# Second SwiGLU and Fourier stage as one pipeline over groups of two batches, with a packed real transform and products on GpSimd

## The reference

```python
# feed-forward of layer 1: SwiGLU, hidden size 384 (weights dequantised by 1/127)
gate = jnp.einsum('bsd,hd->bsh', x, wg)
up = jnp.einsum('bsd,hd->bsh', x, wu)
h = jax.nn.silu(gate) * up
return jnp.einsum('bsh,dh->bsd', h, wd)
...
# attention of layer 2: over frequencies; it adds its own (normalised) input again
fk = jnp.fft.rfft(k, axis=-1)
fk = fk / (jnp.abs(fk) + EPS)
fq = jnp.fft.rfft(q, axis=-1)
fq = fq / (jnp.abs(fq) + EPS)
fv = jnp.fft.rfft(v, axis=-1)
fkv = jnp.cumsum(fk * fv, axis=-2)
values_hat = jnp.fft.irfft(fkv * jnp.conj(fq), n=D, axis=-1)
return x + values_hat
```

## Time and profile before

| what | us |
|---|---|
| median of the runs | 2327.8 |
| lowest and highest of 3 runs | 2325.37, 2330.94 |
| time of the profiled execution | 2331.32 |
| its span | 2329.6 |
| its granted clock, mean | 0.954 |
| the second SwiGLU and the Fourier stage in it | 816.9 to 1038.7 |

### The profile page before, as it was taken

The page is one execution under the profiler, slowest core; times in us unless marked ns, Lnnn a source line. Parts: engine busy times, 40 slices in busy tenths (PEclk is TensorE's granted clock), DMA queues, the critical chain, the costliest instruction groups (busy, mean ns, idle before and its releaser), DMA issues. The chain is left out here.

```text
span 2329.6 us, 66565 instructions
## 1 busy us (share of the span) xinstructions
PE 2085.3 (90%) x21573; PEld 1237.6 (53%) x21573; DVE 1814.9 (78%) x4556; ACT 1460.6 (63%) x3730; POOL 695.9 (30%) x1221
## 2 busy tenths in 40 slices
PE   5999999987899887756999999999999888888798
PEld 4777777755355454542545555555555444444355
DVE  7878877755689647986889998899999877776564
ACT  3565555632488723322878888888888777777331
POOL 2111111100343101322434434434433355552110
PEclk9999999998799988776999999999999999999899
DMA  5000000000434100003343443444344333331000
GB/s 164 2 2 2 2 2 2 2 1 15 137 124 128 40 1 1 1 0 97 121 129 124 129 131 124 128 132 131 128 129 132 113 98 111 98 102 53 1 19 19
DMA packets 198398, 167.48 MB, mean 72 GB/s; under 512 B 15445, under 2 KB 178198, under 8 KB 198198
## 3 DMA queue, kind: packets, MB, share of 16 engines
q1 hardware_dynamic: 198198, 164.90, 22.4%
HBM read 85.42 MB, written 77.63 MB: 70 GB/s over the span
## 5 line engine op out<-in xcount | busy, mean ns | idle before, releaser
L831 DVE TENSOR_REDUCE a_rowmax<-a_psS 128x2 f32<-128x512 f32 x1536 | 964.1, 681 | 141.4 <-PE a_psS L596 137.0
L754 ACT ACTIVATE a_probs<-a_psT 128x512 f32<-128x512 f32 x1536 | 830.5, 601 | 228.9 <-PE a_psT L603 228.8
L596 PE MATMUL a_psS<-stackk,stackq 49*128 49x256 bf16 x3072 | 498.2, 278 | 46.6 <-DMA stackq<-a_negmaxT 14.2
L603 PE MATMUL a_psT<-stackq,stackk 51*128 51x256 bf16 x3072 | 481.9, 273 | 2.1 <-ACT a_probs L754 1.9
L645 PE MATMUL a_psO<-a_probs,values 128*32 128x256 f32 x6144 | 412.8, 386 | 1.4 <-ACT a_probs L754 1.4
L596 PEld LDWEIGHTS a_psS<-stackk,stackq 49*128 49x128 bf16 x3072 | 220.1, 95 | 296.8 <-DVE a_rowmax L831 116.5
L645 PEld LDWEIGHTS a_psO<-a_probs,values 128*32 128x32 f32 x6144 | 160.8, 109 | 144.8 <-issue 51.2
L1175 ACT ACTIVATE a_probs<-a_psS,a_negmax 128x256 f32<-128x256 f32 x256 | 121.1, 473 | 182.8 <-DVE a_negmax L1199 182.8
L603 PEld LDWEIGHTS a_psT<-stackq,stackk 51*128 51x128 bf16 x3072 | 216.9, 94 | 19.3 <-ACT a_probs L754 8.1
L1059 POOL TENSOR_TENSOR a_vr<-a_v,a_rsum 128x256 f32<-128x256 f32 x128 | 79.8, 623 | 392.3 <-DVE a_rsum L1260 371.9
L953 POOL COPY a_xcur<-xT 128x256 f32 (+1 forms) x80 | 31.7, 396 | 467.8 <-ACT values L778 371.7
(11 more groups left out here) (305 smaller groups left out, 3892.6 us busy)
## 6 DMA issues: line engine op xcount, KB each, us to landing
a_scratch<-a_parts SPq DMA_DIRECT2D x192, 192.0 KB, 2.4
stackq<-a_scratch SPq DMA_DIRECT2D x192, 192.0 KB
stackk<-a_scratch SPq DMA_DIRECT2D x192, 192.0 KB
a_scratch<-a_parts SPq DMA_DIRECT2D x192, 128.0 KB, 2.3
a_scratch<-a_parts SPq DMA_DIRECT2D x192, 64.0 KB, 1.9
stackq<-a_negmaxT SPq DMA_DIRECT2D x192, 8.0 KB
x<-in_x SPq DMA_DIRECT2D x4, 512.0 KB, 6.4
out<-x SPq DMA_DIRECT2D x8, 256.0 KB, 2.3
```

The lines of the kernel that those rows point to most:

```text
L596: return pe.matmul(psS[score_bank(s, u)[0]][:, t * SEQ:(t + 1) * SEQ], stackq[r:r + MAX_ROW, b, pr, t * P:(t + 1) * P], stackk[r:r + MAX_R ...
L603: return pe.matmul(psT[shifted_bank(s, u)[0]][:, t * SEQ:(t + 1) * SEQ], stackk[r:r + ZERO_ROW, b, pr, t * P:(t + 1) * P], stackq[r:r + ZE ...
L754: act.activation(probs[:, h, :], psT[shifted_bank(s, u)[0]][:, :], ACT.Exp, scale=of(s, off).exp_scale).then_inc(exp_done, 1)
L831: dve.tensor_reduce(rowmax[:, s.parity(1), u, :], psS[score_bank(s, u)[0]][:, :].rearrange("p (t k) -> p t k", t=2), AX_X, ALU.max).then_i ...
```

## The change

swiglu "f1" and fourier_attention are replaced by one stage, swiglu_fourier, that works on groups of two batches in 12 rounds. In round k all engines work on up to five groups: group k's gates, group k-1's down projection, statistics and second normalisation, group k-2's projection and squares, group k-3's units, products and running sums, and group k-4's last product, back transform and second addition.

Parts of it:
- The statistics of the second normalisation are taken per group: stats1 (VectorE), moment and refine (GpSimd, 12 instructions on 128x4), the root (ScalarE), invert2 (VectorE). Before, they were taken once for all tiles.
- The transform is packed: 65 real columns and the 63 imaginary ones that are not zero, 128 together, in two halves of 64 whose first columns hold the two ends. k, q and v take 384 columns of a PSUM bank.
- q is transposed twice, once shifted by 64 columns, so that both products with the running sum are over 128 partitions. GpSimd makes both (finals); no sum is taken on VectorE or GpSimd, since the signs and sums are in the back transform's weights.
- GpSimd also adds the normalised tokens to x (add_tokens) and copies the two end frequencies' squares (ends).
- gate and up have one PSUM bank each, where they had two. The normalised tiles lie in the weights of attention64, which are free by then.

```diff
-                    pe.matmul(psV[:, 256:256 + 2 * FREQS], m.fold_in[:, k - 3, :], m.dft[:, :], start=True, stop=True, skip_group_check=True)
+                    pe.matmul(psV[:, 256:256 + D], m.fold_in[:, k - 3, :], m.dft[:, :], start=True, stop=True, skip_group_check=True)
...
-def fourier_attention(nc, m, w):
...
+def swiglu_fourier(nc, m, wf, w):
+    HALF = D // 2
+    LAST = GROUPS + 3
...
+        gate, up, misc, psP, psQ, psX, psC = pb("gate"), pb("up"), pb("misc"), [pb("psP0"), pb("psP1")], pb("psQ"), pb("psX"), pb("psC")
...
+            def gates(g, c):
+                if c == 0:
+                    pe.wait_ge(kept1, g + 1)
+                if g or c:
+                    pe.wait_ge(hidden_ready, HCH * g + c)
+                pe.matmul(gate[:, :], wf.gate[:, c * P:(c + 1) * P], m.xT8[:, g, :], start=True, stop=True)
+                pe.matmul(up[:, :], wf.up[:, c * P:(c + 1) * P], m.xT8[:, g, :], start=True, stop=True).then_inc(projected, 1)
...
+            turn1(0)
+            for k in range(LAST + 1):
+                if has(k - 2):
+                    turn2(k - 2)
+                    project(k - 2, 0)
+                if has(k):
+                    gates(k, 0)
+                if has(k - 4):
+                    back(k - 4)
+                if has(k - 1):
+                    down(k - 1)
+                if has(k - 2):
+                    project(k - 2, 1)
+                if has(k - 3):
+                    turn_q(k - 3)
+                if has(k):
+                    gates(k, 1)
+                if has(k + 1):
+                    turn1(k + 1)
+                if has(k - 3):
+                    running_sums(k - 3)
+                if has(k):
+                    gates(k, 2)
...
+            keep1(0)
+            for k in range(LAST + 1):
+                if has(k - 1):
+                    activate(k - 1, 2)
+                if has(k - 2):
+                    keep2(k - 2)
+                    take(k - 2, 0)
+                if has(k):
+                    activate(k, 0)
+                if has(k - 2):
+                    take(k - 2, 1)
+                if has(k - 3):
+                    keep_q(k - 3)
+                if has(k):
+                    activate(k, 1)
+                if has(k + 1):
+                    keep1(k + 1)
+                roots(k - 1, k - 2)
+                if has(k - 3):
+                    keep_total(k - 3)
...
+            def moment(g):
+                v = small[:, g % 2, :, :]
+                mean, dif, var, root, rstd, tmp, guarded, both = (v[:, n, :] for n in range(8))
+                st = m.stats4[:, g, :, :]
+                wait_alone(pool, stats1_done, g + 1, pool_passed)
+                if g >= 2:
+                    wait_alone(pool, xb_ready, g - 1, pool_passed)
+                pool.tensor_tensor(dif, st[:, :, 1], st[:, :, 4], ALU.subtract)
+                pool.tensor_tensor(both, st[:, :, 1], st[:, :, 4], ALU.add)
+                pool.tensor_tensor(var, st[:, :, 2], st[:, :, 5], ALU.add).then_inc(moments, 1)
+                wait_alone(pool, moments, 3 * g + 1, pool_passed)
+                pool.tensor_tensor(tmp, dif, dif, ALU.mult)
+                pool.tensor_scalar(mean, both, 0.5, None, ALU.mult)
+                pool.tensor_scalar(var, var, 1.0 / D, LN_EPS, ALU.mult, ALU.add).then_inc(moments, 1)
+                wait_alone(pool, moments, 3 * g + 2, pool_passed)
+                pool.tensor_scalar(tmp, tmp, 0.25, None, ALU.mult).then_inc(newton, 1)
+                wait_alone(pool, newton, 4 * g + 1, pool_passed)
+                pool.tensor_tensor(guarded, var, tmp, ALU.add).then_inc(moments, 1)
...
+            def refine(g):
+                v = small[:, g % 2, :, :]
+                mean, dif, var, root, rstd, tmp, guarded, both = (v[:, n, :] for n in range(8))
+                wait_alone(pool, inverted2, g + 1, pool_passed)
+                pool.tensor_tensor(tmp, rstd, rstd, ALU.mult).then_inc(newton, 1)
+                wait_alone(pool, newton, 4 * g + 2, pool_passed)
+                pool.tensor_tensor(tmp, tmp, guarded, ALU.mult).then_inc(newton, 1)
+                wait_alone(pool, newton, 4 * g + 3, pool_passed)
+                pool.tensor_scalar(tmp, tmp, -0.5, 1.5, ALU.mult, ALU.add).then_inc(newton, 1)
+                wait_alone(pool, newton, 4 * g + 4, pool_passed)
+                pool.tensor_tensor(rstd, rstd, tmp, ALU.mult).then_inc(rstd_ready, 1)
...
+            def finals(g):
+                wait_alone(pool, total_kept, g + 1, pool_passed)
+                wait_alone(pool, q_kept, 2 * g + 2, pool_passed)
+                if g >= 1:
+                    wait_alone(pool, back_ready, g, pool_passed)
+                for i in range(2):
+                    pool.tensor_tensor(final[:, i, :, :], total[:, :, :], qT[:, :, i, :], ALU.mult).then_inc(final_ready, 1)
+
+            for k in range(LAST + 1):
+                if has(k - 4):
+                    finals(k - 4)
+                if has(k - 2):
+                    add_tokens(k - 2)
+                if has(k - 2):
+                    ends(k - 2)
+                if has(k - 1):
+                    moment(k - 1)
+                    refine(k - 1)
...
+            def units(g):
+                a = sections(kqv[:, g % 2, :, :])
+                dve.wait_ge(inverse_done, 2 * g + 2)
+                if g >= 1:
+                    dve.wait_ge(q_turned, 2 * g)
+                over = lambda i, c: inverse[:, :, i, 1:HALF].unsqueeze(2).to_broadcast([P, 4, c, HALF - 1])
+                dve.tensor_tensor(qunit[:, :, 0:2, 0], a[:, :, Q, :, 0], inverse[:, :, 1, 0:FREQS:HALF], ALU.mult)
+                dve.tensor_tensor(qunit[:, :, 2, :], a[:, :, Q, 0, :], inverse[:, :, 1, 0:HALF], ALU.mult)
+                dve.tensor_tensor(qunit[:, :, 0:2, 1:HALF], a[:, :, Q, :, 1:HALF], over(1, 2), ALU.mult).then_inc(q_unit, 1)
+                dve.tensor_tensor(a[:, :, K, :, 0], a[:, :, K, :, 0], inverse[:, :, 0, 0:FREQS:HALF], ALU.mult)
+                dve.tensor_tensor(a[:, :, K, :, 1:HALF], a[:, :, K, :, 1:HALF], over(0, 2), ALU.mult).then_inc(k_unit, 1)
...
+            for k in range(LAST + 2):
+                if has(k - 1):
+                    gated(k - 1, 2)
+                if has(k - 3):
+                    guard(k - 3)
+                    invert(k - 3, 0)
+                if has(k):
+                    gated(k, 0)
+                if has(k - 3):
+                    invert(k - 3, 1)
+                if has(k + 1):
+                    normalise1(k + 1)
+                if has(k - 4):
+                    update2(k - 4)
+                if has(k - 3):
+                    units(k - 3)
+                if has(k - 1):
+                    update1(k - 1)
+                    stats1(k - 1)
+                if has(k - 3):
+                    products(k - 3)
+                if has(k - 2):
+                    powers(k - 2)
+                if has(k):
+                    gated(k, 1)
+                if has(k - 4):
+                    stats2(k - 4)
+                if has(k - 1):
+                    invert2(k - 1)
+                    normalise2(k - 1)
...
-        swiglu(nc, m, "f1", m.ffn[1])
-        fourier_attention(nc, m, m.fa)
+        swiglu_fourier(nc, m, m.ffn[1], m.fa)
...
-    dft = np.concatenate([np.cos(angle), -np.sin(angle)], axis=1)
-    dft[:, FREQS] = 0.0
-    dft[:, 2 * FREQS - 1] = 0.0
+    cos, sin = np.cos(angle), -np.sin(angle)
+    dft = np.concatenate([cos, sin[:, 1:D // 2]], axis=1)
     weight = np.where((f == 0) | (f == FREQS - 1), 1.0, 2.0)[:, None] / D
-    idft = np.stack([weight * np.cos(angle.T), -weight * np.sin(angle.T)], axis=1)
-    idft[0, 1, :] = 0.0
-    idft[FREQS - 1, 1, :] = 0.0
+    re, im, none = weight * cos.T, weight * sin.T, np.zeros((1, D))
+    inner = slice(1, D // 2)
+    idft = np.stack([np.concatenate([re, re[inner]]), np.concatenate([none, -im[inner], none, im[inner]])], axis=1)
```

More of the change, by code:

```diff
@@ new lines, in normalise2, with gated @@
+            def normalise2(g):
+                dve.wait_ge(rstd_ready, g + 1)
+                if g >= 2:
+                    dve.wait_ge(turned2, g - 1)
+                    dve.wait_ge(xb_added, g - 1)
+                for k in range(4):
+                    last = dve.tensor_scalar(xb[:, g % 2, k, :], m.x4[:, g, k, :], small[:, g % 2, 0, k:k + 1], small[:, g % 2, 4, k:k + 1],
+                                             ALU.subtract, ALU.mult)
+                last.then_inc(xb_ready, 1)
+            def gated(g, c):
+                n = HCH * g + c
+                dve.wait_ge(silu_ready, n + 1)
+                if c == 0 and g >= 2:
+                    dve.wait_ge(out_ready, g - 1)
+                dve.tensor_tensor(hidden[:, g % 2, c, :], silu[:, n % 2, :], up[:, :], ALU.mult).then_inc(hidden_ready, 1)
@@ new lines, in _ @@
+            statistics()
+            normalise1(0)
+            for k in range(LAST + 2):
[28 more added lines that the diff above has]
+                    normalise2(k - 1)
```

419 lines of the change are left out of this document (247 added, 172 removed).

## The result

The changed kernel's median is 2333.7 us over nine runs (2327.9 to 2337.6), that of the kernel before, run beside it on the same chip, 2326.9. The ratio is 1.0032 with a 95% interval of 1.0019 to 1.0046: 6.8 us slower, where 24 us of gain were forecast and the range ended at 2324.

A forecast was written before the change was run, and what follows sets the result against it. Middle rounds of 21.8 us were taken as VectorE's own work plus waits at the seam; start and 12 rounds sum to 197.8 against 221.8 us, 24 gained: 2304 on the runs' scale, range 2290 to 2324.

The forecast's parts named there:

- D: End of a middle round: normalise2 (VectorE) and finals (GpSimd), freed together, exclude each other; 1.1 us a round added.
- A: Head of a middle round, from normalise2's end through TensorE's turning, projection, gate and up to gated(k,0): 5.2 us, VectorE idling 2.3.
- C: After stats2: invert2, four GpSimd instructions in a chain (1.4 us), then normalise2; 2.8 us, VectorE idling 1.5.
- Rival 3: TensorE at the low clock: rounds of about 23 or 25 us, total 2312 or 2326; chance 0.16 for 2316 to 2332.
- B: Middle of a round, from gated(k,0) to stats2: VectorE's own work without a wait, TensorE keeping ahead, 12.7 us.
- The ramps: Fill and drain, us: start 6.0, rounds 0 to 2 12.6, 12.3, 15.7; round 8 16.5, 9 to last 11.0, 9.8, 7.6.
- rival 4: Slower: the second norm hangs on twelve small GpSimd instructions; at 0.6 to 0.9 us each 2328 to 2345; chance 0.09.
- the 0.6 that I had named as a sign: Sign in the new profile: the prediction is wrong if small GpSimd instructions exceed 0.6 us.
- rival 2: A ScalarE table switch costs twice, so silu's copy slips about 1.5 us a round past A's start: 2316; chance 0.05.
- My estimate of 170 for a perfect overlap: Both old stages, TensorE 166 and VectorE 167 busy of 221.8 us: overlapped, near 170 if neither engine waits.

The follow-up runs named there:

- finals_wait: Changed kernel, with GpSimd's final products waiting until the second normalisation (normalise2) is done: 2314.7 us, ratio 0.9940.
- fills: Changed kernel plus 16 matmuls of 128 columns that nobody reads ahead of turn2 in rounds 2 to 9: 2318.1 us, ratio 0.9969.
- wait_and_fills: finals_wait plus unread matmuls: 12 at the start, 8 ahead of each turn2, 12 ahead of back in the last two rounds: 2302.5 us, ratio 0.9884.
- packed_separate: Second SwiGLU left as before the change, then a separate Fourier stage with packed transform and final products on GpSimd: 2303.0 us, ratio 0.9906.

## Why the prediction was wrong
**D, the exclusion, was mis-sized.** I named the place and the pair, and added "one GpSimd instruction", 1.1. But the normalisation is four instructions and the products are two, back to back: the first of the four waited out the first product and the second the second. That is 2.05 in rounds 3 to 8, where I had 1.1. For the second product I wrote that it would fall into A's slack. It does not, since A cannot begin before the normalisation ends. What I wrote of add_tokens held: the guard took 1.22 us beside it (0.43 in finals_wait), inside VectorE's wait in A.

**A failed, and of a middle round's excess this is the larger part.** I priced it at 5.2 with rows of a SwiGLU group at full clock. It took 7.8 (939.32 to 947.13). The seam is serial, so TensorE stands still for most of C and D, 3.77 us, and then makes A, the only stretch in which everything waits for it, at the lower clock. Rival 3 had the mechanism, but I spread the low clock over a round by TensorE's busy share: 0.79, "no colder" than before. The measured mean is 0.81, so that figure was good and of no use. What counts is where the low clock lies: 0.62 in A, 1.00 in the middle of the round, where TensorE has slack. With fills A is 5.3 (912.13 to 917.41), with finals_wait 5.3 (906.17 to 911.45).

**D feeds A.** Without the collision the pause before A is 1.45 us, and in two of the three middle rounds the clock stays up. This is why finals_wait gave some 4.7 us in such a round and not 2.05. In the prediction the two were separate rivals with prices that add; they are one mechanism.

**B and C held.** B was 12.7 and took 11.2 (922.90 to 934.09): its rows add up to 12.4, but each begins some 0.1 before the one ahead of it ends, and I had added them one by one. Of C's 2.8, GpSimd's chain let VectorE idle 1.56 to 1.85 (forecast 1.5). The round: A 7.8 + B 11.2 + C and D 5.2 (934.09 to 939.26) = 24.2, forecast 21.8.

**The ramps were too cheap.** Measured from one end of normalise2 to the next, the start with rounds 0 and 1 took 31.6 (817.7 to 849.3), forecast 30.9. But round 2 took 19.2 (15.7), round 8 21.6 (16.5), and rounds 9, 10 and the last 38.4 (28.4). From 1021 to 1035 the clock is 0.50, with TensorE busy 7.7 of 14.0 us: I had priced rounds with little TensorE work by rows at full clock. Over the stage: middle rounds 4 to 6 were 7.5 over, rounds 3 and 7 4.2, round 2 3.5, and rounds 8 to 11 15.1, which with 0.7 at the start make up the miss of 30.9 (228.7 against 197.8). So more than half of the miss lies outside the middle rounds. The clock accounts for about half of the last 10: rounds 9 to the end take 38.2 in finals_wait and 32.9 in wait_and_fills, at a granted clock of 0.68 and 0.90. The other half, 32.9 against 28.4, stays open.

**Right:** the small GpSimd instructions do not decide (rival 4). They take 0.2 us alone and, five of the twelve, 0.27 to 0.38 at the median beside VectorE's products (two single ones took 0.64 and 0.75, over the 0.6 that I had named as a sign); least, median and greatest ns of three of them and of the last:
```profile
L1820 POOL TENSOR_TENSOR ff_small<-stats x8: 197/374/377, 843.9 to 1000.1; 128x4 f32<-128x4 f32 x8
...
L1824 POOL TENSOR_TENSOR ff_small<-ff_small x8: 197/272/746, 844.6 to 1001.4; 128x4 f32<-128x4 f32 x8
...
L1842 POOL TENSOR_TENSOR ff_small<-ff_small x8: 198/198/199, 848.0 to 1004.6; 128x4 f32<-128x4 f32 x8
```
Table loads cost no more than their 1.28 (rival 2): in the seam above the load begins 0.02 after the copy ends, and silu 0.02 after the load. The wrong side came in by another door than the one I had watched.

**What the prediction did not ask.** It compared the new stage with the old two, never with the change's own parts. The packed stage on its own, with groups of two batches and GpSimd's share of the work, brings 191.4, against 222.0 before. There the SwiGLU takes 8.3 us a group by TensorE's work and the Fourier part 10.8 by VectorE's, 19.0 together. The merged round is 19.4 even when nothing disturbs it, by my reading because its ring of handoffs is as long as the two stages' work; on top come four rounds of filling and draining. So merging gains nothing here, and as it was made it costs 37 us of stage (228.7 against 191.4) and 31 of the medians (2333.7 against 2303.0). With the collision gone and fills in both, 7 us of stage and 11 of the medians are left (190.6 against 183.5, 2302.5 against 2291.1). My estimate of 170 for a perfect overlap needed engines that do not wait for each other. The ring was known from A to D: 5.2 + 12.7 + 2.8 = 20.7 a round, the exclusion aside. The same rows give 8.3 for a SwiGLU group and, as worked out for packed_separate, 11.7 for a separate Fourier group, 20.0 together, so they showed no gain from merging.

Open: how much of the 19.4 a different order of TensorE's list could save. A round with normalise2 taken a round earlier, which would break the ring, was not tried.

## What to carry to other kernels
Price a serial seam at the clock that TensorE may have there: after 3.8 us of standing still it ran at half speed exactly where all others waited for it, while the mean clock looked harmless. Before two stages are merged, compare the length of the new round's ring with the sum of the separate stages' periods, and try the cheaper half of the change alone. When GpSimd takes work over from VectorE, what matters is which VectorE instruction stands beside it: next to reciprocals it was free, next to the normalisation that everyone waits for its 2.5 us cost some 4.7 a round.

## What the runs showed of the hardware that was not expected
- VectorE's four normalisations (128x128, one input in SBUF) took 3.16 us for 1.11 beside two GpSimd products in a row, in 6 of the 8 groups (once 3.06): the first took 1.43 and the second 1.30, each until one product was done, and the last two 0.34 each.
- One GpSimd product of 128x512 takes 1.26 us here, least and greatest 1.26 too, where the earlier trace rows had 1.16 for a bf16 output.
- 16 idle matmuls of 128 columns in a round, 3.73 us of TensorE's time, took 18 us out of a stage of 229.
- A rotation back of 16 matmul rows took 3.47 us after TensorE had stood for 4.89, and 2.05 after 2.25 (granted clock 0.66 from 961 to 966 in the first case).
